# Post-LN transformer layer on one core: high part of x1 first, first layer-norm statistics one slot later, and a maximum ahead of gate and up

## The reference, cut to what matters

```python
# x: [16, 256, 256] fp32: 16 sequences of 256 tokens, width 256
def attn(x):                                   # 16 heads of 16, 4 groups of keys and values
    qkv = x @ Wqkv + bqkv
    scores = einsum('bqhd,bkhd->bhqk', q, k) / 16
    return (softmax(scores) @ v) @ Wout + bout
def ffn(x):                                    # weights are made ternary per group of 64
    gate, up = split(x @ ternary(w_gate_up).T) # 2 x 1024
    h = silu(gate) * up
    return rms_norm(h) @ ternary(w_proj).T
x1  = layernorm(x + attn(x))
out = layernorm(x1 + ffn(x1))
```

## Time and profile before

| what | value |
|---|---|
| median of three runs | 613.4 us (611.0 to 614.56) |
| profiled execution, its own time | 612.37 us |
| its span in the profile | 610.5 us |
| busy share of the span | PE 91%, DVE 71%, ACT 61%, POOL 57% |
| chain of waits, by engine | PE 71%, DVE 15%, issue 5%, DMA 3%, POOL 2% |
| mean granted TensorE clock | 0.968 |

### The profile page before, as it was taken

How to read it: one execution, slowest core, us unless ns; L and a number is a source line. 1 busy time by engine, 2 the same in 40 slices (tenths; PEclk the granted TensorE clock), 3 DMA queues, 4 the chain that set the end, 5 groups by cost and what they waited for, 6 DMA issues and landing times.

```text
span 610.5 us, 14163 instructions
## 1 busy us (share of the span) xinstructions
PE 557.7 (91%) x4368; PEld 471.0 (77%) x4368; DVE 434.5 (71%) x1018; ACT 370.4 (61%) x738; POOL 345.9 (57%) x452
## 2 busy tenths in 40 slices
PE   5688999999999999999999999999999999999782
PEld 5677787778888888878787888888888877777672
DVE  6865866677778777777868777877777677855751
ACT  4444845666666666667575666766666666566441
POOL 4565761244736455555547374636555555566975
PEclk9687999999999999999999999999999999999986
DMA  6955265353353517160725344353517160101001
GB/s 215 152 134 70 77 93 111 57 102 66 78 106 79 105 47 139 45 129 16 156 28 130 52 99 84 77 104 73 109 45 137 39 127 3 37 2 37 19 0 35
DMA packets 53933, 49.08 MB, mean 80 GB/s; under 512 B 6145, under 2 KB 53889, under 8 KB 53889
## 3 DMA queue, kind: packets, MB, share of 16 engines
q1 hardware_dynamic: 51152, 47.60, 37.8%
q10 hardware_dynamic: 2736, 0.92, 0.7%
HBM read 33.29 MB, written 14.68 MB: 79 GB/s over the span
## 4 chain that ended last, share of the span: by engine, by line
PE 71%; DVE 15%; issue 5%; DMA 3%; POOL 2%; ACT 1%; ACTq 1%; SPq 1%; POOLq 0%; DVEq 0%
PE ffn_ps L460 17%; PE short_ps L460 11%; PE pv_ps L557 10%; PE short_ps L507 9%; PE exp_ps L516 7%; PE down_ps L542 7%; PE short_ps L565 5%; DVE gated L831 2%; DVE st L907 2%; PE ffn_ps L581 2%; DVE r L904 2%; DVE x1T_lo L778 2%; DVE row_max L789 2%; DVE h_f L838 1%; DMA wgu_raw<-in_L_ffn_w_gate_up_dram 1%
## 5 line engine op out<-in xcount | busy, mean ns | idle before, releaser
L789 DVE TENSOR_REDUCE row_max<-short_ps 128x2 f32<-128x512 f32 x256 | 174.0, 682 | 68.6 <-PE short_ps L507 68.4
L942 POOL TENSOR_TENSOR h_lo<-h_f,h_hi 128x256 fp32r<-128x256 f32 x128 | 94.8, 741 | 191.1 <-ACT h_hi L685 180.7
L703 ACT ACTIVATE probs<-exp_ps 128x1024 f32<-128x1024 f32 x128 | 131.1, 1024 | 35.5 <-PE exp_ps L516 33.4
L460 PE MATMUL ffn_ps<-x1T_hi,wguT 128*128 128x256 f32 x480 | 125.1, 293 | 16.2 <-DVE h_f L838 9.0
L507 PE MATMUL short_ps<-k_st,q_st 65*128 65x256 f32 x512 | 117.6, 312 | 9.2 <-DVE row_max L789 5.5
L460 PE MATMUL ffn_ps<-x1T_lo,wguT 128*128 128x256 f32 x480 | 119.5, 282 | 0.0
L694 ACT ACTIVATE tanh<-ffn_ps 128x256 f32<-128x256 f32 x120 | 45.9, 383 | 119.7 <-PE ffn_ps L460 103.0
L460 PEld LDWEIGHTS ffn_ps<-x1T_hi,wguT 128*128 128x128 f32 x480 | 90.9, 189 | 23.2 <-DVE h_f L838 11.0
L507 PEld LDWEIGHTS short_ps<-k_st,q_st 65*128 65x128 f32 x512 | 83.2, 194 | 19.2 <-DVE row_max L789 6.9
L460 PEld LDWEIGHTS ffn_ps<-x1T_lo,wguT 128*128 128x128 f32 x480 | 90.9, 189 | 0.0
L947 POOL TENSOR_TENSOR sq_sum<-sq_sum,h_sq 128x256 f32<-128x256 f32 x112 | 83.4, 744 | 0.0
(11 more groups left out here) (100 smaller groups left out, 907.7 us busy)
## 6 DMA issues: line engine op xcount, KB each, us to landing
q_st<-q_dram SPq DMA_DIRECT2D x128, 128.0 KB, 4.0
q_dram<-q_p SPq DMA_DIRECT2D x16, 512.0 KB, 3.0
xn<-in_L_attn_x_dram SPq DMA_DIRECT2D x16, 256.0 KB, 4.4
k_st<-k_dram SPq DMA_DIRECT2D x64, 64.0 KB, 2.6
res<-in_L_attn_x_dram SPq DMA_DIRECT2D x16, 256.0 KB, 3.1
out_dram<-y_out SPq DMA_DIRECT2D x16, 256.0 KB, 2.2
wgu_raw<-in_L_ffn_w_gate_up_dram SPq DMA_DIRECT2D x8, 256.0 KB, 7.2
k_dram<-k_p SPq DMA_DIRECT2D x16, 128.0 KB, 3.1
```

Of the source, the lines that this page charges most:

```text
L460: last = pe.matmul(dst, a, b, start=start and i == 0, stop=stop and i == len(pairs) - 1)
L703: act.activation(probs[:, st.s % 4], exp_ps[:], ACT.Exp).then_inc(exp_done, 1)
L789: dve.tensor_reduce(row_max[:, st.par, head * TT:(head + 1) * TT], short(n, f"max{i}")[:].rearrange("p (t k) -> p t k", t=TT), AX.X, ALU.m ...
L942: pool.tensor_tensor(h_p[1][:, st.s % 4, :], h_f[:, st.s % 2, :], h_p[0][:, st.s % 4, :].bitcast(F32), ALU.subtract).then_inc(h_lo, 1)
```

## The change

- `gate_up` waits at its head for the high part of x1 alone. The four matmuls with the high part (two of gate, two of up) come first, then a wait for the low part, then the four with the low part. The number and the size of the matmuls stay.
- `LN1_STATS = 28`: DVE's statistics of the first layer norm leave slot 3, where they stood right behind the sum `r1`, for slot 4, behind `h_f` and ahead of the second maximum. `RSTD1` goes from 27 to 28 on POOL, where it now stands between `h_lo` and `sq_sum`.
- `RSTD2` goes from 42 to 43, `LN2_APPLY` and `STORE` from 44 to 45: POOL's second root from slot 2 to slot 3, `y_out` and its store from slot 4 to slot 5.
- `MAX_FIRST = 5`: in slot 5 PE issues the first maximum ahead of gate and up.

```diff
+MAX_FIRST = 5
-LN2_APPLY = 44
-STORE = 44
+LN2_APPLY = 45
+STORE = 45
-RSTD1 = 27
+LN1_STATS = 28
+RSTD1 = 28
-RSTD2 = 42
+RSTD2 = 43
             def gate_up(n, st):
-                wait(pe, x1T_lo, st.count(1, 1))
+                wait(pe, x1T_hi, st.count(1, 1))
...
-                for half in range(2):
-                    c = half * F + st.s * P
-                    last = products(gate_up_bank(n, st, half),
-                                    [wguT[:, k, c:c + P] for k in range(DT) for _ in range(2)],
-                                    [x1T[a][:, st.par, k, :] for k in range(DT) for a in range(2)])
+                for a in range(2):
+                    if a:
+                        wait(pe, x1T_lo, st.count(1, 1))
+                    for half in range(2):
+                        c = half * F + st.s * P
+                        first = a == 0 and (half == 0 or alternate(n, st))
+                        for k in range(DT):
+                            last = pe.matmul(gate_up_bank(n, st, half), wguT[:, k, c:c + P], x1T[a][:, st.par, k, :],
+                                             start=first and k == 0, stop=a == 1 and k == DT - 1,
+                                             skip_group_check=True)
...
             def slot(n):
-                if st := n.chunk(FFN0):
+                if (st := n.chunk(FFN0)) and n.t % SLOTS != MAX_FIRST:
                     gate_up(n, st)
...
                     max_scores(n, st, 0)
+                if (st := n.chunk(FFN0)) and n.t % SLOTS == MAX_FIRST:
+                    gate_up(n, st)
...
+                if st := n.once(LN1_STATS):
+                    wait(dve, r1_done, st.count(1, 1))
+                    for t in range(TT):
+                        dve.bn_stats(st1[:, t, :], r1[:, t, :]).then_inc(bn1_done, 1)
+                    wait(dve, bn1_done, st.count(TT, TT))
+                    dve.sem_inc(waited, 1)
+                    for t in range(TT):
+                        dve.bn_aggr(mv1[:, t, :], st1[:, t, :]).then_inc(var1_done, 1)
                 if st := n.once(X1_LOW):
```

More of the change, by code:

```diff
@@ L904, in slot @@
                     dve.tensor_tensor(r1[:], both(n, "o"), res[:, st.par], ALU.add).then_inc(r1_done, 1)
[L905 to L911, removed]
                 if st := n.once(K_LOW):
@@ L943, in slot @@
                                        h_p[0][:, st.s % 4, :].bitcast(F32), ALU.subtract).then_inc(h_lo, 1)
+                if st := n.once(RSTD1):
+                    wait(pool, var1_done, st.count(TT, TT))
+                    pool.tensor_tensor(ve1[:], mv1[:, :, 1], ln_eps[:], ALU.add).then_inc(ve1_done, 1)
+                    wait(pool, ve1_done, st.count(1, 1))
+                    rsqrt(rstd1[:], ve1[:], rstd1_done)
+                if st := n.chunk(H_LOW0):
                     if st.s:
@@ L955, in slot @@
                                           ALU.subtract, ALU.mult).then_inc(y_done, 1)
[L956 to L960, removed]
                 if st := n.once(ADD_BOUT):
```

## The result

The changed kernel takes 622.2 us, the median of four runs (620.8 to 624.4), against 612.2 us for the kernel before on the same chip (four runs, 610.7 to 614.6). The ratio is 1.0177, with a 95% interval of 1.0146 to 1.0207: 10 us slower. The forecast was 618.5 us. The direction and the links in the loop were right, and 4 of the 10 us were missing.

What follows compares the result with a forecast made beforehand. PE sets the pace, with two stops a batch, for `h_f` and `x1T_lo`. 612.37 + 1.2 + 4.6 - 0.7 = 617.5 us profiled, plus 1.0 for the median: 618.5 us, own range 615.5 to 622, 8 in 10 from 607 to 625.

Steps and rivals of the forecast that it cites:

- Part 1: Statistics moved to slot 4: `x` starts 1.54 us later, PE's transposes of x1 0.64 us late, bounds 0.21 and 0.88.
- Part 2: First maximum in slot 5 fills 0.24 us of PE's stop for `h_f`; stop moves to x1's transposes, grows to 0.8 us.
- Part 3: High part first in gate and up: gives back 0.55 of the 0.64 us, leaving a stop of 0.09 for the low part.
- parts 1 to 3: Late statistics, maximum first and high part first together: +0.09 us a batch over 13 batches, +1.2 us, bounds -4.4 and +4.3.
- Part 4: `y_out` and store a slot later: 2.9 us later, SP's x loads delayed, PE stops at transposes of x, +4.6 us.
- Rival 4: PE's granted clock falls in the longer stops, of about 0.8 us in slots 1 and 5; chance 3 in 100.
- Part 5: First batch and last two: shifts under 0.4 us of both signs, fewer POOL operations at the very end, -0.7 us.
- Sum: Whole profiled execution: 612.37 + 1.2 + 4.6 - 0.7 = 617.5 us; median 1.0 higher, so forecast 618.5 us, 0.8% slower.

## Why the prediction was right, and where it was too small

**Part 1, statistics late.** Right, link by link. DVE idle ahead of `x`, for the root: 0.50 us, forecast 0.6. The pair `x`: 1.05 us to the next start, forecast 1.10 between bounds of 0.65 and 1.32. Lateness of the transposes: from the projection of the same batch to them 9.10 us against 8.53, +0.57, forecast +0.64. The statistics late alone cost 0.62 us a batch. On the pair `x`, which has POOL's `sq_sum` beside its first half (335.57 to 336.30): it takes 1.05 us here, 0.65 with POOL idle. The Trainium skill, "SBUF — State Buffer", section "SBUF: two separate sides", has POOL and a DVE instruction that runs in a two-port mode or has two SBUF inputs exclude each other on their shared ports for a whole instruction. The trace agrees with that reading: POOL started 0.07 us earlier, and the first `x` takes 0.81 us and ends at 336.45, 0.15 behind the end of `sq_sum`, as the prediction had let it end, while the second takes 0.40. But the profile shows only durations, not who held what, nor in which mode `x` ran.

**Part 2, maximum first.** Right. Alone it wins 0.24 us a batch (forecast of what it fills: 0.24), and with the statistics late PE arrives early at the transposes and waits there: 0.53 us, 0.63 with the 0.10 by which the matmuls behind a stop come late, forecast 0.8.

**Part 3, high part first.** Right. It gives back 0.52 of the lateness (forecast 0.55) and leaves a stop of 0.12 (0.09). The net of parts 1 to 3 was forecast as +0.09 us a batch; with `y_out` back the loop measures +0.06. Alone, the three edits measure +0.62, -0.57 and -0.24, in sum -0.19. The high part first is worth in company nearly what it is worth alone, and goes to cover the delay of the statistics; what is lost in company, 0.25 a batch, is the gain of the maximum first, since PE waits at the transposes anyway. Over whole runs the parts seem to add: -11.0 for both edits on PE, +11.2 for the statistics, +10.2 for `y_out` and its store make +10.4, and the whole change cost 10.0. That is luck: 3.0 us more are lost with the first two together (+3.2, not +0.2), and the late store costs 3.4 less in company (6.8), which fits the 0.36 us by which `y_out` and the store come earlier there in each of ten batches. The change as a whole holds an 11 us gain (both edits on PE) and gives it away.

**Part 4, the store.** The mechanism was right: 2.7 us later (forecast 2.9), SP's list late, stops at the loads, and the store behind the load takes all of it away. The term was a little small. The stops sum up to 5.4 us, not 4.6: of the three early loads, which I let just fit, two stop for 0.2 to 0.3 us, and the seven in the loop give 4.9. And behind the longest stop the clock fell, 1.75 us more.

**Rival 4** was this last piece. I wrote that I see no row that would make the clock fall, and gave it 3 in 100. I had looked at the new stops that I forecast at about 0.8 us, in which it indeed didn't fall (13 of them, measured at 0.53 to 0.67, none with a lower clock), but I had forecast a stop of 1.4 us in Part 4 myself and did not ask the question of that one. The measured one was 1.36. Nor did I ask it of the filling of the pipeline, where the clock fell behind a stop of 1.03 us.

**Part 5, start and end.** This is the term that failed most: wrong in sign, -0.7 forecast. Both kernels without the late store are 3.2 us slower than before, of which the steady period has 0.8, so what lies outside it costs about 2.4, a miss of 3.1. It comes with the late statistics: the run with them alone has 3 us outside its period too, while the three runs with edits on PE alone lie within 0.8 us of what their period gives over 13 batches. In the tail there is no other batch to fill PE's stops, and the last transposes of x1 wait directly for `x`:

```profile
587.10 0.96 PE L573 MATMUL short_ps<-ident,x 128*128 128x128 f32 x4 [3.73 <-DVE x L913]
```

against 1.75 us before; part of that stop takes the place of others of the kernel before, for `h_lo` and `x1T_lo`. DVE sits idle for 1.08 us ahead of that last `x` for the root, where it sat 0.33 before. I had counted POOL's instructions at the end and not the chain from the root to the transposes, which in the tail has nothing to hide behind; that this chain makes the cost there is my reading of the trace, and no run tests it. How the cost divides between start and tail I can't settle: over the profiled executions of these kernels the second batch's transposes of x1 lie anywhere from 2.3 us ahead (high part first alone) to 2.9 us behind (statistics late alone) those of the kernel before.

**Sum.** Forecast 1.2 + 4.6 - 0.7 = 5.1 us over the profiled execution of before. By the batches it was 1.7 + 5.4 + 1.75 from the second batch to the fourteenth, and 3.3 at start and end, of which about 1.5 is the stretch of lower clock behind 85 us. Neither the kernel before nor the run with `y_out` back has that stretch; the runs with the statistics late alone and with both maxima first have it. The medians differ by 10.0. Two of the misses are of the clock, and of those only one execution of each kernel tells: how much of the 10.0 they make is not shown.

## What to carry to other kernels

A store that waits at the head of an in-order issue list delays every load behind it: before moving the step that a store waits for, look for the loads behind it and the cover that each has, and put the store behind them. An edit that removes a wait is worth what the trace shows only if the engine that it waited for is not made later in the same change: test the halves alone, since here one half held a gain of 11 us and the other spent it. Work out the filling and the emptying of a pipeline as chains of their own, since a delay that the steady loop covers stands open there. And whoever forecasts a stop should ask of each single one, not of the mean, what the clock does behind it.

## What the runs showed of the hardware

- PE's granted clock fell from 2.4 to 1.2 GHz in the middle of the program behind stops of 1.36 us (kernel after) and 1.42 us (late `y_out` alone), for about 3.4 us (worked out from the two-microsecond rows above), which in the kernel after cost 1.75 us; behind stops of 1.24, 1.11 and 1.05 us of the run with late `y_out` alone and the 13 of 0.53 to 0.67 us it did not. The length of the stop doesn't decide it: at about 85 us the clock fell behind a stop of 1.03 us (kernel after) and one of 0.70 us (statistics late alone), and at the same place it stayed at 2.4 GHz behind one of 1.09 us (both edits on PE). What decides it these runs don't show.
- After each stop PE is another 0.10 us late: the second matmul behind it starts 0.22 us after the first, where neighbours are 0.12 apart, whether the stop was 0.26 us long (run with the maximum first alone, 291.43 to 291.65) or 0.50 (kernel before, 293.98 to 294.20).
